# A two-layer attention and mixture-of-experts kernel: all loops written out, and four steps of the first attention moved between engines and places

## The chip, the cores and the metric

The kernel runs on one core of a Trainium2 chip. The metric is the time of one execution in device microseconds (us); less is better. Engines are called as in the profile: PE (TensorE; PEld are its weight loads), DVE (VectorE), ACT (ScalarE), POOL (GpSimd) and SP (SyncE, which here only issues DMAs).

## The reference, cut to what matters

The input is x of 16 batches x 512 tokens x 128 columns, in fp32. Two layers follow each other; a layer adds an attention and an expert network, both of the normalised x, to x.

```
xn = layernorm(x)
h  = rmsnorm(xn) * w;  q, k = l2norm(h Wq), l2norm(h Wk);  v = h Wv        # 4 heads, 2 kv heads, 32 columns
a0 = xn + gate * (softmax(causal(temperature * q k^T)) v) Wo
e0 = xn + sum over the 2 best of 16 experts: weight * (gelu(xn W1 + b1) W2 + b2)
x  = x + a0 + e0
xn = layernorm(x)
q, k, v = rmsnorm(xn) Wq, Wk, Wv, q and k times a rotary factor            # 16 heads, 4 kv heads, 8 columns
a1 = s + s Wo,   s = softmax(q k^T / sqrt(128)) v
e1 = the best of 8 experts: (silu(xn G) * (xn U)) D
x  = x + a1 + e1
```

## The kernel before, in words

`build` runs six stages one after the other, with a barrier between them: `setup`; `layer0_attention` (to about 490 us in the trace); `group_table`, a short stage that turns the counts of tokens for each expert into a table of groups of 256 rows; `expert_ffn` for layer 0 (80 groups, to about 681 us); `layer1_attention` (to about 1660 us); a second `group_table`; and `expert_ffn` for layer 1 (40 groups, to the end). Tokens reach their expert by indirect DMAs that POOL issues.

**Order.** Each engine has its own program, written by hand; semaphores tie them together (`wait_ge`, `then_inc`). In the attention stages a `body(i, o)` does one batch, and inside it the work of later batches is woven in: `o + 1` stands for the next batch, `o + 2` for the one after it. `bodies` (L196) calls it: batches 0 to 2 written out, then a loop of 5 turns with two batches in each (3 to 12), then batches 13 to 15 written out. In the loop the wait values are worked out in registers. `expert_ffn` does the same by `pipeline`: 8 groups written out, a loop of 8 turns (layer 0) or 3 turns (layer 1) with 8 groups in each, the last 8 groups written out. SP's loads there have a loop of their own. `passed` (L73) adds a semaphore increment, an instruction of its own, between waits, and `Chain.link_apart` (L62) is `link` with such an increment behind its wait.

**First attention, one batch, by engine.** Times and lines of one period stand in the rows below.

- DVE: `normalise` of the batch before (L450, L452), `statistics` of o+2 (L345, L348), `add_output` of the batch before (L459), `heads_rows` of o+1 (q, k, v rows, L380 to L387), `choose` of o+1 (routing, L393 to L408), `kz_rows` of o+1, `normal_rows` of o+2 (L357), `slots` of o+1 (L424 to L443, the last writes `meta`), `keep_sum` (L366), `square_sums` of o+2 (L372).
- POOL: `factors` of o+1 (L529 to L534), four scatters of batch o (`scatter(o, 1)`, L544), `norms` of o+2 (L512 to L518), four scatters of o+1 (`scatter(o + 1, 0)`). A scatter needs `meta` of its batch.
- PE: score pairs 0, 1, 2 (`scores`, L695 and L698; eight to a batch, two banks in turn, so pair u waits for the exponentials of pair u-2), `output` of the batch before (L723), values 0, score pair 3, `q_columns` of o+1, score pair 4, `k_columns` of o+1, values 1, `ranks` of o+1 (L671, L672), score pair 5, `x_rows` of o+2, score pair 6, the first `project`, values 2, score pair 7, two projects, values 3, the last project. `q_columns`, `k_columns`, `x_rows` and `output` all use the PSUM bank `ps_t`.
- ACT: the exponentials of the eight pairs (L607), `qT_copy` of o+1 behind the fourth (L593), `odds` of o+1 (L599) behind the fifth, `xT_copy`, four `prj_copy` and `squares` (L586) of o+2 between and behind the rest.

`kz_rows` takes the transposed keys out of `ps_t`: four copies of 32 partitions x 512 columns, each head in its own rows. `x_rows` of the next batch waits for it (`kT_sb`), and so do the scores of that batch.

**Second attention.** 64 score tiles and 64 tiles for the row maxima in a batch on PE (L1806, L1834), maxima on DVE (L1605), exponentials on ACT (L1511).

**Expert network of layer 0.** ACT does for each group two Gelus (L1078), the store of the group before (L1087), and the load of the weights of the group eight later (L1082), whose row it reads from the table. PE does the matmuls (L1047, L1057).

Of the kernel before, what the change touches and what calls it, by code (L numbers as in the profile page):

```python
# [10 lines left out]
ALU = mybir.AluOpType  # L11
# [32 lines left out]
class Chain:  # L44
# [14 lines left out]
    def link_apart(self, ins):  # L59

        self.n += 1
        ins.then_inc(self.sem, 1)  # L62
        self.eng.wait_ge(self.sem, self.base + self.n)
        passed(self.eng, self.passed)

    def end(self):
        assert self.n == self.per, (self.sem, self.n, self.per)


def passed(eng, count):  # L70


    eng.sem_inc(count, 1)  # L73
# [143 lines left out]
def layer0_attention(nc, k, x_d, base_d, meta_d, xs_d):  # L217


    with ExitStack() as ctx:  # L220
# [72 lines left out]
        with nc.Block() as block:  # L293

            @block.sync
            def _(sp):
                def load(i, o):
                    b, h, p = batch(i, o)
                    sp.wait_ge(x_used, b + 1)
                    passed(sp, k.passed_sp)  # L300
                    sp.dma_start(x[:, p], x_d[bass.ds(b * L, L), :].rearrange("(t p) d -> p t d", p=P)).then_inc(x_in[p], 16)

                def store_meta(i, o):
                    b, h, p = batch(i, o)
                    sp.wait_ge(meta_ready, b + 1)
                    passed(sp, k.passed_sp)
                    sp.dma_start(meta_d[bass.ds(b * P, P), :], meta[:, p]).then_inc(meta_out[p], 16)

                def store_base(i, o):
                    b, h, p = batch(i, o)  # L310
                    sp.wait_ge(wo_used, b + 3)
                    passed(sp, k.passed_sp)
# [21 lines left out]
            def _(dve):  # L334
# [4 lines left out]
                def statistics(i, o):  # L339
# [6 lines left out]
                    ln.link_apart(last)  # L346
# [43 lines left out]
                def choose(i, o):  # L390

                    b, h, p = batch(i, o)
                    heads.link_apart(nc.vector.tensor_tensor(lg[:], prj[:, :, QKV0:PRJ0],  # L393
# [3 lines left out]
                    heads.link_apart(last)  # L397
# [11 lines left out]

                def kz_rows(i, o):  # L410

                    b, h, p = batch(i, o)
                    dve.wait_ge(kT_ps, b + 1)
                    for head in range(H0):
                        r = slice(head * DH0, (head + 1) * DH0)
                        last = nc.vector.tensor_copy(kz[r, p, head, :], ps_t[r, :])
                    last.then_inc(kT_sb, 1)
# [44 lines left out]
                def body(i, o):  # L462
# [24 lines left out]
                kz_rows(0, 0)  # L487
# [10 lines left out]
            def _(pool):  # L498
# [3 lines left out]
                def norms(i, o):  # L502
# [8 lines left out]
                    passed(pool, k.passed_pool)  # L511
# [3 lines left out]
                    ln.link_apart(nc.gpsimd.tensor_tensor(tmp4[:, 2], tmp4[:, 1], mv[:, :, 1], ALU.mult))  # L515
# [5 lines left out]
                def factors(i, o):  # L521
# [7 lines left out]
                    fc.link_apart(nc.gpsimd.tensor_tensor(ftmp[:, 0], ss[:], bc, ALU.mult))  # L529
# [8 lines left out]
                def scatter(i, o, c):  # L538
                    b, h, p = batch(i, o)
                    if c == 0:  # L540
                        pool.wait_ge(meta_ready, b + 1)
                        passed(pool, k.passed_pool)
# [5 lines left out]
                def body(i, o):  # L548
# [12 lines left out]
                scatter(0, 0, 0)  # L561
                bodies(pool, body)
# [4 lines left out]
            def _(act):  # L567
# [26 lines left out]

                def odds(i, o):
# [14 lines left out]
                def body(i, o):  # L610
# [6 lines left out]
                    if nxt:  # L617
# [1454 lines left out]
```

## Time and profile before

| what | us |
|---|---|
| median of 3 runs (lowest, highest) | 1857.05 (1851.42, 1863.5) |
| the profiled execution, its own time | 1872.54 |
| its span, first to last instruction | 1870.8 |
| PE busy in the span | 1590.7 (85%) |
| DVE busy | 1231.6 (66%) |
| ACT busy | 939.0 (50%) |
| POOL busy | 831.1 (44%) |

Busy shares are means over stages with different limits, so the stages are read apart. Matmuls are pipelined and their ends are modelled, so a busy PE is not PE at its peak. PEclk is the granted clock as a share of 2.4 GHz.

### The profile page before, as it was taken

How to read it: one execution, taken by the hardware profiler on the slowest of the kernel's cores; microseconds unless marked ns; L12 is line 12 of the kernel's file. 1: busy time of each engine (PE TensorE's matmuls, PEld its weight loads, DVE VectorE, ACT ScalarE, POOL GpSimd, SP SyncE). 2: the span in 40 equal slices, each digit the busy share in tenths (PEclk: the TensorE clock that was granted, in tenths of full speed). 3: DMA queues.
4: the chain of work that ended last, by engine and by line, in shares of the span. 5: the costliest groups of instructions: out<-in, count | busy, mean ns of one | idle time of the engine just before them, and what ended most of it. 6: DMA issues, size and time to landing. Idle time of an engine off the chain costs nothing. (4 is left out here: it accounts for less than half of the span.)

```text
span 1870.8 us, 35103 instructions
## 1 busy us (share of the span) xinstructions
PE 1590.7 (85%) x9488; PEld 825.8 (44%) x9488; DVE 1231.6 (66%) x3176; ACT 939.0 (50%) x1790; POOL 831.1 (44%) x987
## 2 busy tenths in 40 slices
PE   1688888888499954899999999999999999928997
PEld 0344444444298852233333333333333333308996
DVE  4466566657333335688888797888878899714443
ACT  1233433434143321577777676776767777712221
POOL 2465566556140024555555555455545541003444
PEclk9999999999799985699999899999999999969998
DMA  2011111111399951212112222122211111028772
GB/s 64 26 38 43 38 39 40 34 45 32 116 279 280 280 157 57 60 55 61 58 53 66 66 58 58 43 63 67 66 57 49 52 57 55 13 62 285 234 240 80
DMA packets 141468, 165.01 MB, mean 88 GB/s; under 512 B 28010, under 2 KB 114154, under 8 KB 140138
## 3 DMA queue, kind: packets, MB, share of 16 engines
q1 hardware_dynamic: 86628, 70.75, 13.1%
q10 hardware_dynamic: 40912, 62.62, 11.1%
q0 software_dynamic: 13824, 30.47, 5.3%
q8 instruction: 39, 0.64, 0.1%
q14 instruction: 65, 0.53, 0.1%
HBM read 111.93 MB, written 51.30 MB: 87 GB/s over the span
## 5 line engine op out<-in xcount | busy, mean ns | idle before, releaser
L1605 DVE TENSOR_REDUCE c_mx<-c_ps_mx 128x1 f32<-128x512 f32 x1024 | 650.4, 684 | 121.9 <-PE c_ps_mx L1834 99.3
L1511 ACT ACTIVATE c_pt<-c_ps_e 128x512 f32<-128x512 f32 x1024 | 557.7, 602 | 230.4 <-PE c_ps_e L1806 222.4
L1834 PE MATMUL c_ps_mx<-c_kex,c_qst 72*128 72x512 bf16 x1024 | 405.7, 399 | 34.1 <-DVE c_mx L1605 20.7
L1806 PE MATMUL c_ps_e<-c_qst,c_kex 74*128 74x512 bf16 x1024 | 396.1, 389 | 1.7 <-ACT c_pt L1511 1.0
L1819 PE MATMUL c_ps_v<-c_pt,c_vp 128*32 128x512 f32 x2048 | 280.6, 621 | 1.1 <-ACT c_pt L1511 0.7
L1834 PEld LDWEIGHTS c_ps_mx<-c_kex,c_qst 72*128 72x128 bf16 x1024 | 101.8, 99 | 355.4 <-DVE c_mx L1605 225.7
L1343 POOL DMA_INDIRECT c_gy<-ys,mt x128 | 124.0, 969 | 295.8 <-issue 161.8
L607 ACT ACTIVATE a_pt<-a_ps_s,temp 128x1024 f32<-128x1024 f32 (+3 forms) x128 | 112.7, 883 | 182.6 <-PE a_ps_s L698 110.4
L1047 PE MATMUL f_ps_h<-f_xT,f_w 128*128 128x256 f32 x800 | 195.5, 384 | 0.0
L695 PE MATMUL a_ps_s<-a_qT,a_kz 128*128 128x128 f32 (+3 forms) x512 | 181.7, 472 | 0.0
L544 POOL DMA_INDIRECT xs<-a_xn,a_meta x128 | 129.2, 1010 | 109.5 <-DVE a_meta L443 75.7
L1047 PEld LDWEIGHTS f_ps_h<-f_xT,f_w 128*128 128x128 f32 x800 | 144.7, 193 | 15.0
L1057 PE MATMUL f_ps_y<-f_w,f_h 128*128 128x128 f32 x1120 | 149.4, 280 | 1.0 <-ACT f_h L1078 0.2
L1057 PEld LDWEIGHTS f_ps_y<-f_w,f_h 128*128 128x128 f32 x1120 | 139.5, 192 | 19.3 <-ACT f_h L1078 12.9
L1441 POOL DMA_INDIRECT rows<-c_row,c_bsl x64 | 63.7, 996 | 158.2 <-PE c_ps_v L1819 127.1
L1806 PEld LDWEIGHTS c_ps_e<-c_qst,c_kex 74*128 74x128 bf16 x1024 | 101.3, 99 | 73.7 <-ACT c_pt L1511 15.0
L1003 POOL DMA_INDIRECT out<-f_y,f_x x80 | 76.6, 957 | 127.3 <-DVE f_y L1130 114.8
L1078 ACT ACTIVATE f_h<-f_ps_h,f_w 128x256 f32<-128x256 f32 x160 | 67.1, 470 | 97.3 <-PE f_ps_y L1057 63.6
L695 PEld LDWEIGHTS a_ps_s<-a_qT,a_kz 128*128 128x128 f32 x512 | 81.5, 198 | 60.9 <-issue 51.4
L1074 ACT ACTIVATE f_g<-f_ps_h 128x256 f32<-128x256 f32 x120 | 46.0, 383 | 118.1 <-PE f_ps_h L1047 98.9
L1134 DVE TENSOR_TENSOR f_y<-f_ps_y,f_w 128x256 f32<-128x256 f32 x80 | 34.0, 425 | 104.8 <-PE f_ps_y L1057 104.8
L1035 PE MATMUL f_ps_x<-ident,f_x 128*128 128x128 f32 x240 | 47.3, 280 | 59.7 <-DMA f_x<-rows 37.7
(231 smaller groups left out, 1990.9 us busy)
## 6 DMA issues: line engine op xcount, KB each, us to landing
f_w<-in_we ACTq DMA_DIRECT2D x80, 321.0 KB, 4.0
f_w<-in_we ACTq DMA_DIRECT2D x40, 576.0 KB
c_qst<-qparts SPq DMA_DIRECT2D x45, 384.0 KB
f_x<-rows SPq DMA_DIRECT2D x40, 257.0 KB
f_x<-xs SPq DMA_DIRECT2D x80, 128.0 KB, 3.9
ys<-f_y ACTq DMA_DIRECT2D x80, 128.0 KB, 3.6
qparts<-c_qp SPq DMA_DIRECT2D x16, 384.0 KB
c_kex<-kparts SPq DMA_DIRECT2D x48, 96.0 KB
```

Of the source, the lines that this page charges most:

```text
L544: nc.gpsimd.indirect_dma_start(xs_d, bass.IndirectOffsetOnAxis(ap=meta[:, p, c * NT + t:c * NT + t + 1], axis=0), xn[:, p, t, :], None).th ...
L607: nc.scalar.activation(pt[:, kt % 2, 2 * pr:2 * pr + 2, 0:n], ps_s[:, u % 2, :, 0:n], ACT.Exp, bias=k.temp[:, 3:4], scale=k.temp[:, 1:2]). ...
L695: nc.tensor.matmul(ps_s[:, u % 2, j, 0:L - kt * P], kz[:, p, head, kt * P:(kt + 1) * P], qT[:, p, kt * P:L], start=True, stop=False)
L1003: nc.gpsimd.indirect_dma_start(ys_d, bass.IndirectOffsetOnAxis(ap=x[:, q, t, 2 * D:ROW].bitcast(U32), axis=0), y[:, q, t, :], None).then_i ...
L1047: last = nc.tensor.matmul(ps_h[u][:, n, :], w[:, q, col:col + P], xT[:, q % 2, :], start=True, stop=True)
L1057: last = nc.tensor.matmul(ps_y[q % 2][:, t * D:(t + 1) * D], h[:, q % 2, c, t * P:(t + 1) * P], w[:, q, col:col + D], start=c == 0, stop=c ...
L1343: nc.gpsimd.indirect_dma_start(gy[:, p, n, :], None, ys_d, bass.IndirectOffsetOnAxis(ap=mt[:, p, n:n + 1], axis=0)).then_inc(gathered[p], 16)
L1511: nc.scalar.activation(pt[:, s % 4, hl, :], ps_e[:, ring_bank(p, n)], ACT.Exp, scale=QSCALE).then_inc(exp_done, 1)
L1605: nc.vector.tensor_reduce(mx[:, g % 2, n % 16:n % 16 + 1], ps_mx[:, ring_bank(p, n)], AX, ALU.max).then_inc(mx_done, 1)
L1806: nc.tensor.matmul(ps_e[:, ring_bank(p, n)], kex[:, p, hl, kt * P:(kt + 1) * P], qst[:, p, HL * g + hl, :], start=True, stop=True).then_in ...
L1819: last = nc.tensor.matmul(ps_v[32 * hl:32 * (hl + 1), :], vp[:, p, kt, hl, :], pt[:, s % 4, hl, :], start=kt == 0, stop=kt == NT - 1)
L1834: nc.tensor.matmul(ps_mx[:, ring_bank(p, n)], qst[0:SROW, p, HL * g + hl, qt * P:(qt + 1) * P], kex[0:SROW, p, hl, :], start=True, stop=Tr ...
```

## The change

Every loop is written out: `bodies` calls all 16 bodies, and `pipeline` and SP's loads in `expert_ffn` are Python loops. The wait values become constants. All calls of `passed` go, and `link_apart` becomes `link`. Four things change in the first attention alone:

```diff
 def bodies(eng, body):
-    for o in range(3):
-        body(0, o)
-    with eng.Fori(1, 6) as i:
-        body(i, 1)
-        body(i, 2)
-    for o in range(13, NB):
+    for o in range(NB):
         body(0, o)
```

DVE's body no longer copies the keys (nor does its start, where `kz_rows(0, 0)` stood behind `choose(0, 0)`); ACT does, behind the fifth exponential and ahead of `odds` (at the start, behind `qT_copy(0, 0)`):

```diff
                         choose(i, o + 1)
-                        kz_rows(i, o + 1)
...
+                def kz_copy(i, o):
+                    b, h, p = batch(i, o)
+                    act.wait_ge(kT_ps, b + 1)
+                    for head in range(H0):
+                        r = slice(head * DH0, (head + 1) * DH0)
+                        last = nc.scalar.activation(kz[r, p, head, :], ps_t[r, :], ACT.Copy)
+                    last.then_inc(kT_sb, 1)
...
                     exps(i, o, 4)
                     if nxt:
+                        kz_copy(i, o + 1)
                         odds(i, o + 1)
```

POOL's body has the norms ahead of all eight scatters of the next batch (at its start, `scatter(0, 0, 1)` now follows `scatter(0, 0, 0)`):

```diff
                     if nxt:
                         factors(i, o + 1)
-                    scatter(i, o, 1)
                     if nxt2:
                         norms(i, o + 2)
                     if nxt:
                         scatter(i, o + 1, 0)
+                        scatter(i, o + 1, 1)
```

PE's body has the output behind four score pairs, and the ranks ahead of values 1:

```diff
-                    for u in range(3):
+                    for u in range(4):
                         scores(i, o, u)
                     if prev:
                         output(i, o - 1)
                     values(i, o, 0)
-                    scores(i, o, 3)
                     if nxt:
                         q_columns(i, o + 1)
                     scores(i, o, 4)
                     if nxt:
                         k_columns(i, o + 1)
+                        ranks(i, o + 1)
                     values(i, o, 1)
-                    if nxt:
-                        ranks(i, o + 1)
                     scores(i, o, 5)
```

In the expert stages, SP's loads and the pipeline of the others:

```diff
-                with sp.Fori(1, n_grp // NBUF) as i:
+                for i in range(1, n_grp // NBUF):
...
-                with eng.Fori(1, last) as i:
+                for i in range(1, last):
```

## Rows read from the trace of the kernel before

**Rows 1.** Window, one period: length, busy PE, PEld, DVE, ACT, POOL, clock, DMA, GB/s.

```profile
286.56:313.73 27.17, 22.27 (x142) 11.29 (x141) 17.20 (x59) 10.31 (x17) 16.19 (x20) 0.94 0.13 39
```

**Rows 2.** Timeline of POOL, that period: start, us, line, [idle before <-releaser].

```profile
278.47 1.09 POOL L544 DMA_INDIRECT xs<-a_xn,a_meta  x1 [4.81 <-DVE a_meta L443]
...
282.39 0.96 POOL L544 DMA_INDIRECT xs<-a_xn,a_meta  x1 [0.30 <-issue]
286.56 0.22 POOL L529 TENSOR_TENSOR a_ftmp<-a_ss,a_r2sq 128x24 f32<-128x24 f32 x1 [3.20 <-DVE a_ss L372]
...
291.61 0.23 POOL L534 TENSOR_TENSOR a_fac<-a_ftmp,a_r 128x24 f32<-128x24 f32 x1
...
297.16 0.23 POOL L512 TENSOR_SCALAR a_tmp<-a_mv 128x4 f32<-128x4 f32 x1
...
300.69 0.20 POOL L518 TENSOR_TENSOR a_r2sq<-a_r 128x4 f32<-128x4 f32 x1
305.53 1.09 POOL L544 DMA_INDIRECT xs<-a_xn,a_meta  x1 [4.64 <-DVE a_meta L443]
```

**Rows 3.** Timeline of DVE in the same period.

```profile
292.38 0.68 DVE L380 TENSOR_TENSOR a_qn<-a_prj,a_fac 128x512 f32<-128x512 f32 x1
...
296.28 0.23 DVE L408 TENSOR_TENSOR a_ohb<-a_oh 128x64 bf16<-128x64 f32 x1
297.72 2.79 DVE L416 COPY a_kz<-a_ps_t 32x512 f32<-32x512 f32 x4 [1.21 <-PE a_ps_t L647]
301.02 1.11 DVE L357 TENSOR_SCALAR a_xn<-a_x,a_mv,a_rstd 128x128 f32<-128x128 f32 x4 [0.51 <-POOL a_r2sq L518]
...
304.54 0.16 DVE L443 CAST a_meta<-a_slotf 128x8 uint32<-128x8 f32 x1
```

**Rows 4.** Timeline of PE in the same period.

```profile
290.51 1.16 PE L723 MATMUL a_ps_t<-wo,a_attnT 128*128 128x128 f32 x8 [1.99 <-DVE a_attnT L452]
...
294.26 0.86 PE L695 MATMUL a_ps_s<-a_qT,a_kz 128*128 128x384 f32 x2
...
302.19 0.66 PE L647 MATMUL a_ps_t<-ident,a_xn 128*128 128x128 f32 x4 [2.08 <-DVE a_xn L357]
```

**Rows 5.** Windows, second attention: written-out batch, over turn's end, last, 13 together.

```profile
875.28:929.34 54.06, 53.03 (x318) 20.10 (x316) 47.94 (x114) 40.57 (x79) 30.36 (x36) 1.00 0.22 62
...
1037.83:1098.80 60.97, 57.38 (x318) 21.25 (x316) 48.53 (x115) 41.00 (x79) 30.33 (x36) 0.92 0.19 55
...
1496.67:1550.43 53.76, 53.01 (x318) 19.84 (x316) 48.31 (x115) 40.54 (x79) 25.62 (x31) 1.00 0.20 59
sum 728.93, PE 703.97 PEld 266.94 DVE 625.55 ACT 529.06 POOL 389.88; mean PE 54.15 PEld 20.53 DVE 48.12 ACT 40.70 POOL 29.99
```

**Rows 6.** Timeline of DVE where the first loop turn of the second attention ends.

```profile
1042.54 1.29 DVE L1605 TENSOR_REDUCE c_mx<-c_ps_mx 128x1 f32<-128x512 f32 x2 [3.46 <-issue]
```

**Rows 7.** Windows, 8 groups, layer 0's experts: first loop turn, third.

```profile
534.40:550.21 15.81, 15.81 (x113) 14.88 (x113) 6.13 (x16) 5.87 (x14) 7.77 (x14) 1.00 0.98 300
...
567.16:584.07 16.91, 16.77 (x113) 14.32 (x113) 6.14 (x16) 6.71 (x16) 0.00 (x0) 1.00 0.97 280
```

**Rows 8.** Window of layer 1's experts, 16 groups in two loop turns.

```profile
1757.70:1824.00 66.30, 66.30 (x418) 61.34 (x417) 32.66 (x80) 18.32 (x49) 30.55 (x33) 1.00 0.76 238
```

**Rows 9.** Timelines: first and last `factors` of the bodies; ACT's copy of `ps_t`.

```profile
71.37 0.22 POOL L529 TENSOR_TENSOR a_ftmp<-a_ss,a_r2sq 128x24 f32<-128x24 f32 x1 [2.40 <-DVE a_ss L372]
...
447.60 0.24 POOL L529 TENSOR_TENSOR a_ftmp<-a_ss,a_r2sq 128x24 f32<-128x24 f32 x1
...
296.11 0.59 ACT L593 ACTIVATE a_qT<-a_ps_t 128x512 f32<-128x512 f32 x1
```

**Rows 10.** Timeline before the first body: routing done, keys copied.

```profile
47.15 0.23 DVE L408 TENSOR_TENSOR a_ohb<-a_oh 128x64 bf16<-128x64 f32 x1
...
50.46 2.79 DVE L416 COPY a_kz<-a_ps_t 32x512 f32<-32x512 f32 x4 [3.09 <-PE a_ps_t L647]
```

**Rows 11.** Instruction queue packets in two written-out batches, 821.5 to 929.34 us.

```profile
q14 instruction: 6, 0.05, 0.2%
```

More of the change, by code:

```diff
@@ L305, in store_meta @@
                     sp.wait_ge(meta_ready, b + 1)
-                    passed(sp, k.passed_sp)
                     sp.dma_start(meta_d[bass.ds(b * P, P), :], meta[:, p]).then_inc(meta_out[p], 16)
@@ L345, in statistics @@
                         last = nc.vector.bn_stats(stats[:, t, :], x[:, p, t, :])
-                    ln.link_apart(last)
+                    ln.link(last)
                     for t in range(NT):
@@ L392, in choose @@
                     b, h, p = batch(i, o)
-                    heads.link_apart(nc.vector.tensor_tensor(lg[:], prj[:, :, QKV0:PRJ0],
+                    heads.link(nc.vector.tensor_tensor(lg[:], prj[:, :, QKV0:PRJ0],
                                                              k.br0[:].unsqueeze(1).to_broadcast([P, NT, E0]), ALU.add))
@@ L396, in choose @@
                         last = nc.vector.max(mx8[:, t, :], lg[:, t, :])
-                    heads.link_apart(last)
+                    heads.link(last)
                     for t in range(NT):
@@ L408, in choose @@
                     nc.vector.tensor_tensor(ohb[:], oh[:, 0], oh[:, 1], ALU.add).then_inc(oh_ready, 1)
[L410 to L417, printed above, removed]
                 def slots(i, o):
@@ L510, in norms @@
                         pool.wait_ge(qkv_ready, b - 1)
-                    passed(pool, k.passed_pool)
                     ln.link(nc.gpsimd.tensor_scalar(tmp4[:, 0], mv[:, :, 1], EPS_LN, None, ALU.add))
@@ L514, in norms @@
                     ln.link(nc.gpsimd.tensor_tensor(tmp4[:, 1], rstd[:], rstd[:], ALU.mult))
-                    ln.link_apart(nc.gpsimd.tensor_tensor(tmp4[:, 2], tmp4[:, 1], mv[:, :, 1], ALU.mult))
+                    ln.link(nc.gpsimd.tensor_tensor(tmp4[:, 2], tmp4[:, 1], mv[:, :, 1], ALU.mult))
                     ln.link(nc.gpsimd.tensor_scalar(tmp4[:, 0], tmp4[:, 2], 1e-6, None, ALU.add))
@@ L528, in factors @@
                     bc = r2sq[:].unsqueeze(2).to_broadcast([P, NT, H0 + KV0])
-                    fc.link_apart(nc.gpsimd.tensor_tensor(ftmp[:, 0], ss[:], bc, ALU.mult))
+                    fc.link(nc.gpsimd.tensor_tensor(ftmp[:, 0], ss[:], bc, ALU.mult))
                     fc.link(nc.gpsimd.tensor_scalar(ftmp[:, 1], ftmp[:, 0], 1e-24, None, ALU.max))
@@ L541, in scatter @@
                         pool.wait_ge(meta_ready, b + 1)
-                        passed(pool, k.passed_pool)
                     for t in range(NT):
@@ L561, in _ @@
                 scatter(0, 0, 0)
+                scatter(0, 0, 1)
                 bodies(pool, body)
@@ L639, in _ @@
                 qT_copy(0, 0)
+                kz_copy(0, 0)
                 rows(1)
@@ L1000, in put_rows @@
                     pool.wait_ge(y_sb, j + 1)
-                    passed(pool, k.passed_pool)
                     for t in range(GT):
@@ L1248, in put_k @@
                     sp.wait_ge(kl_ready, b + 1)
-                    passed(sp, k.passed_sp)
                     sp.dma_start(kparts_d[p].rearrange("j r l -> r j l"), kp[:]).then_inc(k_out[p], 16)
@@ L1254, in put_q @@
                     sp.wait_ge(ql_ready, b + 1)
-                    passed(sp, k.passed_sp)
                     sp.dma_start(qparts_d[p].rearrange("j r l -> r j l"), qp[:]).then_inc(q_out[p], 16)
@@ L1275, in q_stack @@
                     sp.wait_ge(q_out[p], 16 * (h + 1))
-                    passed(sp, k.passed_sp)
                     for a in range(3):
@@ L1295, in shift @@
                     sp.wait_ge(sh_ready, 4 * b + g + 1)
-                    passed(sp, k.passed_sp)
                     for n in range(2):
@@ L1340, in gather @@
                         pool.wait_ge(pv, 16 * (b - 3) + s + 2)
-                    passed(pool, k.passed_pool)
                     for n in rows:
@@ L1369, in norms @@
                     ln.link(nc.gpsimd.tensor_tensor(tmp4[:, 1], rstd[:], rstd[:], ALU.mult))
-                    ln.link_apart(nc.gpsimd.tensor_tensor(tmp4[:, 2], tmp4[:, 1], mv[:, :, 1], ALU.mult))
+                    ln.link(nc.gpsimd.tensor_tensor(tmp4[:, 2], tmp4[:, 1], mv[:, :, 1], ALU.mult))
                     ln.link(nc.gpsimd.tensor_scalar(tmp4[:, 0], tmp4[:, 2], float(np.finfo(np.float32).eps), None, ALU.add))
@@ L1400, in k_parts @@
                     pool.wait_ge(kT_sb, b + 1)
-                    pc.link_apart(nc.gpsimd.tensor_tensor(kr[:], k32[:], kp[:, 0, :], ALU.subtract))
+                    pc.link(nc.gpsimd.tensor_tensor(kr[:], k32[:], kp[:, 0, :], ALU.subtract))
                     pc.link(nc.gpsimd.tensor_copy(kp[:, 1, :], kr[:]))
@@ L1407, in q_parts @@
                     pool.wait_ge(qT_sb, b + 1)
-                    pc.link_apart(nc.gpsimd.tensor_tensor(qr[:], q32[:], qp[:, 0, :], ALU.subtract))
+                    pc.link(nc.gpsimd.tensor_tensor(qr[:], q32[:], qp[:, 0, :], ALU.subtract))
                     pc.link(nc.gpsimd.tensor_copy(qp[:, 1, :], qr[:]))
@@ L1418, in normal_rows @@
                         pool.wait_ge(kept_xn, b - 1)
-                    passed(pool, k.passed_pool)
                     for t in range(NT):
@@ L1429, in keep_xn @@
                     pool.wait_ge(xn_ready, b + 1)
-                    passed(pool, k.passed_pool)
                     nc.gpsimd.tensor_copy(row[:, p, :, 0:D], xn[:, p]).then_inc(kept_xn, 1)
@@ L1439, in scatter @@
                         pool.wait_ge(pv, 16 * (b + 1) + s + 2)
-                    passed(pool, k.passed_pool)
                     nc.gpsimd.indirect_dma_start(
@@ L1653, in choose @@
                     dve.wait_ge(prj_sb, NT * (b + 1))
-                    passed(dve, k.passed_dve)
                     lg = prj[:, :, QKV1:PRJ1]
@@ L1657, in choose @@
                         last = nc.vector.max(mx8[:, t, :], lg[:, t, :])
-                    pro.link_apart(last)
+                    pro.link(last)
                 def choose_index(i, o):
@@ L1696, in statistics @@
                         last = nc.vector.bn_stats(stats[:, t, :], x1[:, p, t, :])
-                    ln.link_apart(last)
+                    ln.link(last)
                 def moments(i, o):
```

16 lines of the change are left out of this document (removed).

## The prediction

> **What bounds the kernel now.** I read the page first, then windows by stage, then the timelines of one period, then the timeline of a turn's end. The chain that ended last reaches back only into the last stage, so it can't say what an edit in the first stages is worth; each stage has to be read by its own period.
>
> In the first attention no engine is full: in a period of 27.17 us PE is busy 22.3, DVE 17.2, POOL 16.2 and ACT 10.3 [rows 1]. So a ring of waits sets the period. The timelines show it. `factors` starts on POOL at 286.56 and ends at 291.84 [rows 2]. On DVE the q rows follow at 292.38, the routing ends at 296.51, then DVE waits 1.21 us for the transposed keys and spends 2.79 us on copying them; the normal rows start at 301.02 (after 0.51 us for POOL's norms), and `meta` is written by 304.70 [rows 3]. POOL's norms, behind four scatters, only ended at 300.89 [rows 2]. After the normal rows PE transposes them, projects, ACT squares, DVE sums, and the next `factors` starts 27.17 us after the last. PE stands still for 1.99 us ahead of the output [rows 4], and its clock is granted at 0.94 on average [rows 1].
>
> In the second attention PE is busy 53.0 of 54.06 us in a written-out batch. In the batch over the end of a loop turn it takes 60.97 us, with 57.4 busy at a clock of 0.92 [rows 5]. DVE stands still there for 3.46 us, and the row names no releaser but "issue" [rows 6]. There are four such turn ends in the stage, and none in the six written-out batches.
>
> In layer 0's experts the first loop turn takes 15.81 us for 8 groups with PE always busy, a later one 16.91 us [rows 7]. In that stage DMA moves 280 to 300 GB/s at a share of 0.97. In layer 1's experts PE is busy all 66.30 us of 16 groups, two turn ends included [rows 8].
>
> **The change part by part.** All sums are against the profiled execution (1872.54 us, span 1870.8), which is 0.8% over the median of 1857.05; I take the gain over unscaled, since the two differ by less than the gain's own doubt.
>
> *1. Key columns by ACT.* Four copies of 32x512 leave DVE: 2.79 us, and with them the wait of 1.21 us ahead of them [rows 3]. ACT gains four. ACT's copy of 128x512 out of the same bank took 0.59 us [rows 9]; on DVE 32x512 cost 2.79 / 4 = 0.70 each, so fewer partitions need not be cheaper. I take 4 x 0.59 = 2.4 us; the ends are 0.8 (four times the 0.2 us of ACT's smallest operations here) and twice my value, 4.7. They lie behind the fifth exponential and ahead of `odds` and the sixth. What hides them is PE's score pair 5, values 1 and the ranks, which PE does between the keys' transposes and `x_rows`; ACT is busy only 10.3 of 27.2 us. If the cover is gone (4.7 us), `x_rows` and `slots` (which needs `odds`) come some 1 to 2 us later.
>
> *2. Norms ahead of the scatters.* POOL's norms take 300.89 - 297.16 = 3.73 us. They needed only statistics that DVE has by the end of `factors`, and now follow `factors` at once: they end at F + 5.3 + 3.8 = F + 9.1 (F is the start of `factors`), instead of F + 14.3. So neither the keys nor the norms hold the normal rows: DVE starts them when routing ends.
>
> *3. The eight scatters in one piece.* The first four take 282.39 + 0.96 - 278.47 = 4.88 us, spaced by 0.96 and 0.30 idle; eight take 2 x 4.88 + 0.30 = 10.06 us [rows 2]. Behind them on POOL's queue stands the next `factors`, and DVE's q rows wait for that. Here the edit can turn against itself, so I add up the ring through POOL: `factors` 5.28; handoff 0.05; q rows to the end of routing 296.51 - 292.38 = 4.13; handoff 0.05; normal rows to `meta` 304.70 - 301.02 = 3.68; handoff to the scatter 305.53 - 304.70 = 0.83; eight scatters 10.06; handoff 0.1. Sum 24.2 us. The removed `passed` increments are worth about 0.1 us each, three of them in this ring; I leave them as margin.
>
> *4. Output behind four pairs, ranks earlier.* Pair 3 is two products of 0.86 us each with two short ones behind them, all overlapping in part, about 1.6 us, and it moves into the 1.99 us in which PE waited for the output's input [rows 4]. It needs the exponentials of pair 1, which are done by then. The values 0 behind it lose nothing. The keys' transposes had ended when DVE began to copy them, at 297.72 or F + 11.2 [rows 3]; 1.6 us earlier is F + 9.6. The ranks now stand ahead of values 1 and wait for the end of routing at F + 9.5, so they cost nothing.
>
> The PE ring: `x_rows` started at 302.19, F + 15.6, after a wait of 2.08 us [rows 4]. PE was ready for it at F + 13.5 and is now at F + 11.9, with the normal rows done at F + 10.7 (they start at F + 9.5 and take 1.1). What follows, to the next `factors`, took 27.17 - 15.6 = 11.5 us, and a mean clock of 0.94 means that 0.06 x 27.17 = 1.6 us of a period are lost to the half clock. That makes 23.4 us, or 21.8 with that loss gone; PE's own busy time of 22.3 is in between. It is shorter than POOL's 24.2, so POOL's ring is late next, and it sets the period.
>
> First attention: from the first to the last `factors` 447.60 - 71.37 = 376.23 us in 14 periods, 26.87 each [rows 9]; at 24.2 that is 338.8, a gain of 37.4. At the start, routing ends at 47.38 and then DVE waited 3.09 us for the keys and copied for 2.79 us before the statistics of batch 1 [rows 10]. Now these start at once: norms end at 53.4, `meta` of batch 0 at 57.1, eight scatters from 57.9 to 68.0, so the second `factors` starts at 68.1 instead of 71.37: 3.3 us. The tail gives 0.7. Sum 41 us.
>
> *5. Loops of the second attention.* 13 batches took 728.93 us; written-out ones took 53.76 to 54.06 (four of them among these, mean 53.9) [rows 5]. 13 x 53.9 = 700.7, so 28 us go, if the new code runs like the written-out code that is there: 3.5 us of standstill at four turn ends, and about as much again of half clock behind each. The upper end is 29; the lower is 0, if what DVE waits for at a turn's end is met once in a batch anyway.
>
> The Trainium skill (Runtime: NRT & Kernel Launch, "Instruction fetch mechanics") says that an engine holds two pages of instructions and fetches ahead in sequence only, so that a taken branch out of them stalls for a fetch, while straight code hides it. The 3.46 us fit. Another page (Advanced Engine Details and Errata, "Control Flow Timing") gives about 0.1 us for a compare-and-branch; by that alone the four turn ends were worth 0.4 us and the sum would be 28 us smaller. The trace speaks for the first.
>
> *6. Loops of layer 0's experts.* Eight turns; the first took 15.81, the other seven about 16.93 each. The first shows that DMA can carry that pace (300 GB/s) [rows 7]. What slows the others is ACT, which does two Gelus and two DMA issues per group with registers worked out between, and is late for PE after the written-out start's lead is used up. 7 x (16.93 - 15.81) = 7.8 us at most, 0 at least (DMA share 0.97); I take 7, nearer to the first turn's row since nothing in it waits for a DMA.
>
> *7. Layer 1's experts.* PE never stands still [rows 8]: 0. Barriers, tables and `setup` are untouched: 0. The other `passed` increments lie beside longer waits: 0.
>
> Sum: 41 + 28 + 7 = 76 us. The profiled execution would go to 1796, the median to 1857 - 76 = 1781 us.
>
> **The rivals.**
>
> *A. The period of the first attention closes elsewhere.* The kz copies on ACT at their dear end, `odds` behind them, PE's in-order wait for the ranks, or half clock on PE keep the period at 26 to 27. For it: the orders of four engines are moved at once, and PE has 22.3 busy of 27. Against it: the sums above. Part 4 and 1 to 3 then give 5 to 15 us instead of 41: 1857 - 35 - 10 = 1812. Chance 0.2.
>
> *B. POOL's ring is not as long as that*, since some of the handoffs overlap, and PE's sets 22.6, the middle of its bounds: 14 x 1.6 = 22 us more, 1759. Against it: every link of the sum is an in-order step. Chance 0.07.
>
> *C. Straight code stalls for its instructions: slower.* Where a loop turn reused what an engine held, written-out code must bring in each piece once, and POOL, DVE or ACT stands still for it in the middle of the chain. For it: the loop code of the first attention and of layer 0's experts ran hundreds of us with next to none of those transfers, and in layer 0's experts they would queue behind a DMA share of 0.97. Against it: the two written-out batches of the second attention brought in 6 packets of instructions on one of the two queues [rows 11] and show no standstill over 0.9 us. Price: one standstill with its half clock is (728.93 - 700.7) / 4 = 7.1 us per attention batch, for 16 to 20 batches that were in loops, and 3.5 us per 8 groups in 11 turns: 20 x 7.1 + 11 x 3.5 = 180 us at most, against 76 won. It decides the sign once some 42% of them lie bare; at 60%, 1781 + 108 = 1889 us. Chance 0.06.
>
> *D. The loops alone give nothing* (the stall at a turn's end only moves to other places, as many as before), while the first attention gains its 41: 1857 - 41 = 1816. For it: the DVE row says "issue", not what it waited for. Against it as for C. Chance 0.07.
>
> **How the numbers follow.** The forecast has 0.6: 1781 us. The range reaches to rivals A and D on one side and nearly to B on the other: 1760 to 1822; outside are C, most of B, and a stall or two in many places. A measurement of this kernel can tell about 1% (18.6 us) from no change. The forecast, A, B and D all lie more than 1% below 1857, though A and D could join: 0.88 faster, 0.06 within 1%, 0.06 slower.
>
> **What would show it.** Right: `factors` of successive batches 24.2 us apart, on POOL directly behind the eighth scatter with no idle for DVE's sums; normal rows directly behind the routing on DVE, with no wait; four ACT copies of about 0.6 us; batches of the second attention all at 53.8 to 54.1 us with a clock of 1.00; the 80 groups 1.97 us apart. Wrong: a period of 26 or more, with the wait ahead of `x_rows` still there; standstills of 3 us with "issue" on DVE or ACT in the middle of written-out bodies; groups at 2.05 us or more, with DMA as releaser.

## The result, and the profile after

| | median us (lowest, highest), runs |
|---|---|
| before | 1854.24 (1850.62, 1863.5), 4 |
| after | 1770.33 (1767.86, 1775.95), 4 |
| ratio after to before | 0.9544, 95% interval 0.9501 to 0.9588 |
| profiled execution after | 1775.95, span 1774.2 |

The kernel became 84 us faster; 1781 had been forecast, inside 1760 to 1822. The time came out nearly right in part by luck: the largest term of the sum, 41 us for the first attention's orders, measured 22 to 25, and the increments, which were put at nothing, measured 25 to 28. The loops were sized rightly.

The period of the first attention, from one `factors` to the next, is now 23.46 us. The window has the columns of [rows 1].

```profile
254.07:277.53 23.46, 20.73 (x145) 11.24 (x143) 14.41 (x55) 12.86 (x21) 16.43 (x19) 1.00 0.15 47
```

POOL's timeline of that period answers to [rows 2].

```profile
254.07 0.24 POOL L496 TENSOR_TENSOR a_ftmp<-a_ss,a_r2sq 128x24 f32<-128x24 f32 x1
...
259.04 0.23 POOL L501 TENSOR_TENSOR a_fac<-a_ftmp,a_r 128x24 f32<-128x24 f32 x1
...
263.33 0.20 POOL L485 TENSOR_TENSOR a_r2sq<-a_r 128x4 f32<-128x4 f32 x1
267.41 1.27 POOL L510 DMA_INDIRECT xs<-a_xn,a_meta  x1 [3.88 <-DVE a_meta L413]
268.98 0.96 POOL L510 DMA_INDIRECT xs<-a_xn,a_meta  x1 [0.30 <-issue]
...
276.56 0.95 POOL L510 DMA_INDIRECT xs<-a_xn,a_meta  x1 [0.30 <-issue]
277.53 0.24 POOL L496 TENSOR_TENSOR a_ftmp<-a_ss,a_r2sq 128x24 f32<-128x24 f32 x1
```

DVE's timeline answers to [rows 3].

```profile
259.30 0.69 DVE L359 TENSOR_TENSOR a_qn<-a_prj,a_fac 128x512 f32<-128x512 f32 x1 [1.08 <-POOL a_fac L501]
...
262.98 0.23 DVE L387 TENSOR_TENSOR a_ohb<-a_oh 128x64 bf16<-128x64 f32 x1
263.56 1.11 DVE L336 TENSOR_SCALAR a_xn<-a_x,a_mv,a_rstd 128x128 f32<-128x128 f32 x4 [0.36 <-POOL a_r2sq L485]
...
266.95 0.16 DVE L413 CAST a_meta<-a_slotf 128x8 uint32<-128x8 f32 x1
...
274.44 0.95 DVE L351 TENSOR_REDUCE a_ss<-a_sq 128x24 f32<-128x768 f32 x1 [6.73 <-ACT a_sq L553]
```

The new `factors` starts as the eighth scatter ends, with no idle, though DVE's sums have been there since 275.39: POOL's ring closes the period. It can be added up in these rows: `factors` and norms up to the normal rows 9.49, normal rows to `meta` 3.55, handoff 0.30, eight scatters 10.10. The keys no longer stand on DVE, and what holds the normal rows is 0.36 us of the norms. ACT's copies:

```profile
263.46 2.37 ACT L568 ACTIVATE a_kz<-a_ps_t 32x512 f32<-32x512 f32 x4
```

PE's timeline of the period ([rows 4]) has three waits left, and none ahead of the output or of `x_rows`; the clock of the window is 1.00.

```profile
261.05 0.66 PE L625 MATMUL a_ps_t<-ident,a_qn 128*128 128x128 f32 x4 [1.77 <-DVE a_v L366]
267.50 0.72 PE L640 MATMUL a_ps_p<-w,a_xnT 128*128 128x272 f32 x2 [0.29 <-ACT a_xnT L539]
271.13 0.70 PE L640 MATMUL a_ps_p<-w,a_xnT 128*128 128x272 f32 x2 [0.58 <-ACT a_prj L547]
```

The other stages, as windows of the same kernel: 8 groups of layer 0's experts; two ordinary batches of the second attention; its one odd batch.

```profile
530.00:545.80 15.80, 15.80 (x114) 14.98 (x113) 6.05 (x17) 6.84 (x16) 0.00 (x0) 1.00 1.02 304
810.40:863.91 53.51, 52.95 (x318) 20.10 (x316) 47.83 (x114) 40.43 (x79) 30.35 (x36) 1.00 0.21 63
...
1023.77:1076.78 53.01, 52.73 (x318) 20.17 (x316) 47.75 (x114) 40.44 (x79) 30.38 (x36) 1.00 0.22 64
1076.78:1135.90 59.12, 57.25 (x318) 21.05 (x316) 48.28 (x115) 40.95 (x79) 29.98 (x35) 0.91 0.20 57
```

The experts answer to [rows 7]: every 8 groups take 15.80 us now, at 304 GB/s. The batches answer to [rows 5]: 53.0 to 53.5 us and no turn's end. In the odd one POOL waits 4.29 us for gathered rows (2.6 on average in the two batches before it), DVE then 1.80 us for POOL, PE 1.59 us for DVE, and the clock falls. Of the nine other kernels below with all loops written out, eight took 53.2 to 54.4 us for the same batch and one 58.4. What delays those rows stays open.

### The profile page after: what moved, and what is told of

Its sections match the earlier page's. It is cut to its first block and busy times, and to the rows that moved or that the text cites. A ratio compares the mean times of both kernels' runs of the same rounds, so it can differ in the third digit from the quotient of the medians.

```text
span 1774.2 us, 29893 instructions
## 1 busy us (share of the span) xinstructions
PE 1545.9 (87%) x9488; PEld 819.9 (46%) x9488; DVE 1183.1 (67%) x3112; ACT 974.2 (55%) x1853; POOL 835.1 (47%) x987
## 5 line engine op out<-in xcount | busy, mean ns | idle before, releaser
L1794 PE MATMUL c_ps_mx<-c_kex,c_qst 72*128 72x512 bf16 x1024 | 401.5, 394 | 17.4 <-issue 8.5
L1766 PE MATMUL c_ps_e<-c_qst,c_kex 74*128 74x512 bf16 x1024 | 392.0, 385 | 1.7 <-ACT c_pt L1472 1.6
L1779 PE MATMUL c_ps_v<-c_pt,c_vp 128*32 128x512 f32 x2048 | 276.7, 612 | 1.1 <-ACT c_pt L1472 0.7
L673 PE MATMUL a_ps_s<-a_qT,a_kz 128*128 128x128 f32 (+3 forms) x512 | 175.3, 461 | 0.0
L1032 PEld LDWEIGHTS f_ps_y<-f_w,f_h 128*128 128x128 f32 x1120 | 144.0, 192 | 6.3
L1032 PE MATMUL f_ps_y<-f_w,f_h 128*128 128x128 f32 x1120 | 144.3, 275 | 0.0
```

The lines of the kernel that those rows point to most:

```text
L673: nc.tensor.matmul(ps_s[:, u % 2, j, 0:L - kt * P], kz[:, p, head, kt * P:(kt + 1) * P], qT[:, p, kt * P:L], start=True, stop=False)
L1032: last = nc.tensor.matmul(ps_y[q % 2][:, t * D:(t + 1) * D], h[:, q % 2, c, t * P:(t + 1) * P], w[:, q, col:col + D], start=c == 0, stop=c ...
L1766: nc.tensor.matmul(ps_e[:, ring_bank(p, n)], kex[:, p, hl, kt * P:(kt + 1) * P], qst[:, p, HL * g + hl, :], start=True, stop=True).then_in ...
L1779: last = nc.tensor.matmul(ps_v[32 * hl:32 * (hl + 1), :], vp[:, p, kt, hl, :], pt[:, s % 4, hl, :], start=kt == 0, stop=kt == NT - 1)
L1794: nc.tensor.matmul(ps_mx[:, ring_bank(p, n)], qst[0:SROW, p, HL * g + hl, qt * P:(qt + 1) * P], kex[0:SROW, p, hl, :], start=True, stop=Tr ...
```

## The experiments

All times are medians, ratios are to runs of the kernel before made on the same chip in the same set (medians 1852 to 1856 us). Single executions of the kernel before spread from 1850 to 1870 us, those of a changed one by 2 to 9, so differences between medians are good to a few us. "Period" is the mean over the fourteen between the second `factors` and the last; the second attention is counted from its first batch's slots to its last batch's.

**The kernel before once more.** Its first profiled execution was 18 us above the median, so I wanted a second profile.

> The kernel before once more, for a second profile. The first profiled execution took 1872.5 us where the median of all is 1855. Theory: what differs is how often PE falls to half clock: the first attention's period is 27.1 us with such a stretch and 25.55 without one, and the first profile has twelve with and two without; at a time near 1855 some ten of fourteen or fewer have one, or the turn ends of the second attention cost less. Rival: the same twelve, and the difference lies in the second attention alone (batches over 59 us).

It took 1852.56 us, and here every second period keeps its full clock. Two successive periods as windows:

```profile
250.17:276.39 26.22, 22.81 (x144) 11.78 (x143) 17.12 (x59) 10.84 (x17) 15.99 (x20) 0.93 0.13 40
276.39:301.32 24.93, 21.19 (x143) 11.07 (x142) 17.19 (x59) 10.41 (x17) 16.20 (x19) 1.00 0.14 42
```

The first `factors` of the bodies is at 71.58 and the last at 430.00: a mean of 25.60 where the profile that I had read has 26.87 [rows 9]. That is 17.8 of the 20.0 us between the two executions; the second attention adds 6.3 (874.9 against 868.6), and what follows it gives 4.7 back. The period that I had taken as typical [rows 1] is one with the clock down, and twelve of fourteen were such; this one, near the median, has seven.

**Loops and increments, each alone.** First the kernel before with every loop written out and the increments gone, orders as before:

```
-    with eng.Fori(1, 6) as i:
-        body(i, 1)
-        body(i, 2)
+    for o in range(NB):
+        body(0, o)
...
-    eng.sem_inc(count, 1)
+    pass
```

> The kernel before with every loop written out and no added increments; the first attention keeps its old orders (keys on DVE, four scatters ahead of the norms, output behind three pairs). Theory: the loops are worth 33 us in the second attention (batches at 53.1) and 8 us in layer 0's experts (groups at 1.97), and in the first attention only the increments in its ring count: periods fall from 26.9 to about 26.4, 7 us. Time about 1854 - 48 = 1806 us. Rival (the loops are most of the change, also in the first attention): periods of 24 or less there and a time of 1780 or less.

1795.82 us, ratio 0.9678 (0.9636 to 0.9721). Period 24.81 (24.44, and 26.01 in the three with a lower clock) where 26.4 had been expected, from the profile with twelve such periods; second attention 834.4, experts 15.80 per 8 groups.

Then the same with the increments kept:

> The kernel before with all loops written out and nothing else: orders as before and every passed increment kept. Theory (loops and increments add up): the second attention's batches at 54.1 to 54.5 us, its thirteen 845 us from first to last, layer 0's experts 15.8 us per 8 groups; in the first attention the period is the 24.4 to 24.8 of the run with loops out and increments gone, plus the 0.75 us that increments cost with the new orders: 25.2 to 25.6. Time 1795.8 + 10 + 11 = about 1817 us. Rival (the turn's end costs the first attention nothing; what shortened its period there was that the increments went): period stays 26.9, so 14 x 1.3 = 18 us more, 1835 us. Second rival (increments hide behind DVE's and PE's waits in the old order): 24.4 to 24.8, 1807 us.

1820.68 us, ratio 0.9786 (0.9731 to 0.9842): the sum of loops and increments nearly as the first theory had it (1817). The second attention took 849.4 us; in the first the period is 25.66 (24.86 and 26.33 in turn), as good as the 25.60 of the second profile of before. So the loops cost the first attention nothing, which was the rival's thesis; its 1835 us came from the period of 26.87.

**The orders alone**, loops and increments kept:

> The kernel before with the four moved steps of the first attention alone; loops and increments stay. Theory: periods of the first attention fall to the sum of POOL's ring with its increments, about 24.2 us, a gain of 41 us, and the other stages stay as before (four turn ends in the second attention, batches of 54): about 1813 us. Rival (the orders pay only with straight code, since the wait values in registers lengthen the handoffs): periods of 25.5 or more, 1830 us or more.

1842.83 us, ratio 0.9934 (0.9909 to 0.9958), where 1813 had been expected. The period is 24.55 (24.01 at best, six of fourteen with a lower clock), not 24.2. The last `factors` is at 411.85 instead of 430.00, but the second attention took 884.4 us instead of 868.6, with batches over a turn's end of 61.4 to 63.7 us instead of 58.6 to 61.2 in the two profiles of before. No instruction of that stage was changed. Why its turn ends became dearer is open. With the loops kept, then, the orders are worth 12 us.

**The changed kernel with all increments back**, then with those of one group of engines:

```
+def passed(eng, count):
+    eng.sem_inc(count, 1)
...
+                    passed(pool, k.passed_pool)
```

> The kernel after with all semaphore increments between waits put back. Theory: the increments are what my sums missed: each costs several tenths of a us where it stands between a wait and the work, so the first attention's period rises from 23.47 to about 24.2 (10 us) and a batch of the second attention from 53.1 to 53.9 (12 us): 1770 + 22 = 1792 us. Rival (they cost about 0.1 us, as the prediction had it, and the constants in place of registers did the rest): 1774 us at most, periods of 23.6 and batches of 53.2.

1798.77 us, ratio 0.9703 (0.9658 to 0.9748): 28 us given back, 22 had been expected. POOL's and DVE's timelines of that kernel around `factors`, `meta` and the first scatters:

```profile
260.64 0.24 POOL L513 TENSOR_TENSOR a_ftmp<-a_ss,a_r2sq 128x24 f32<-128x24 f32 x1
261.07 0.28 POOL L514 TENSOR_SCALAR a_ftmp<-a_ftmp 128x24 f32<-128x24 f32 x1 [0.20 <-POOL a_ftmp L513]
...
274.70 1.09 POOL L528 DMA_INDIRECT xs<-a_xn,a_meta  x1 [4.42 <-DVE a_meta L429]
276.10 0.96 POOL L528 DMA_INDIRECT xs<-a_xn,a_meta  x1 [0.30 <-issue]
```

```profile
273.72 0.16 DVE L429 CAST a_meta<-a_slotf 128x8 uint32<-128x8 f32 x1
```

From the end of `meta` to the second scatter it is 276.10 - 273.88 = 2.22 us, and 268.98 - 267.11 = 1.87 without increments. From the first operation of `factors` to the second it is 0.43 and 0.33 (254.07 to 254.40). The period is 24.00 to 24.04 in eleven of fourteen.

> The changed kernel with the passed increments back on POOL alone. In the run with all of them back, meta to the second scatter took 2.22 us instead of 1.87, factors and norms 0.1 us more each, and two of 0.1 us on DVE lay in the 0.36 us that DVE waits for the norms. Theory (those of POOL are the ones that cost): period 24.0 us, + 8 us in the first attention, the second attention's batches at 54 us like with all of them, about 1795 us. Rival (the costs are spread over the three engines): period 23.7, batches at 53.5, 1782 us.

> The changed kernel with the passed increments back on SP and DVE and none on POOL. Theory: DVE's two lie in its wait for the norms and SP's loads are early, so the period stays at 23.47 to 23.5 and the second attention at 53.1 to 53.4 a batch: 1770 to 1774 us. Rival (DVE's chain in the second attention is PE's supplier, SP's reloads of k and q stand in it): batches 53.6 to 54, 1778 to 1785 us.

POOL alone: 1797.8 us, ratio 0.9697 (0.9661 to 0.9733). SP and DVE alone: 1771.98, ratio 0.956 (0.9526 to 0.9594). So the whole 28 us are POOL's, and those of the other two cost nothing that shows. In the second attention the waits of DVE say how; over three batches with POOL's increments:

```profile
DVE c_mx L1600 <- PE c_ps_mx L1829: 13.8, 30, 0.8
DVE c_stats L1691 <- POOL c_x L1353: 2.3, 3, 1.2
```

and with those of SP and DVE, the same three batches:

```profile
DVE c_mx L1600 <- PE c_ps_mx L1829: 13.7, 30, 0.8
```

The columns are us in total, times, longest. POOL's combined rows `c_x` come late once a batch, 0.77 us each time; DVE waits for them in order ahead of the maxima that PE waits for. A batch there takes 53.55 to 54.24 us where it takes 53.22 to 53.45 without.

**One turn's end instead of four.** Before, with only two loop turns in each attention:

```
-    with eng.Fori(1, 6) as i:
+    with eng.Fori(1, 3) as i:
         body(i, 1)
         body(i, 2)
-    for o in range(13, NB):
+    for o in range(7, NB):
         body(0, o)
```

> The kernel before with batches 3 to 6 in two loop turns and 7 to 12 written out, in both attentions: one turn end in each where the kernel before has four, registers and increments as before, and the loops of the experts as before. Theory (the cost is the turn's end, not the registers): second attention first to last 875 - 3 x 7 = about 853 us, one batch of 59 to 61 us, the looped ones without a turn's end 54.1 to 54.5; first attention between 26.9 and the 25.7 us of the run with loops out. Time about 1855 - 21 - 9 = 1825 us. Rival (written-out code stalls as often for its instructions): 1850 to 1856 us. Second rival (working out addresses in registers is what costs): the written-out batches 53.5 and below, the looped ones 54.5 and above.

1835.52 us, ratio 0.9904 (0.9869 to 0.9939). Windows of the second attention: a looped batch inside a turn, the one over the turn's end, two behind it; below, DVE's row at the turn's end.

```profile
961.26:1015.44 54.18, 52.97 (x318) 20.09 (x316) 47.87 (x115) 40.33 (x78) 30.37 (x36) 1.00 0.22 63
1015.44:1076.65 61.21, 57.33 (x318) 21.35 (x316) 48.53 (x115) 41.06 (x79) 30.34 (x36) 0.92 0.19 55
1076.65:1130.75 54.10, 52.96 (x318) 20.10 (x316) 47.87 (x115) 40.67 (x79) 30.38 (x36) 1.00 0.21 62
1130.75:1184.52 53.77, 53.02 (x318) 19.91 (x316) 48.01 (x114) 40.55 (x79) 30.37 (x36) 1.00 0.22 63
```

```profile
1020.20 1.29 DVE L1605 TENSOR_REDUCE c_mx<-c_ps_mx 128x1 f32<-128x512 f32 x2 [3.51 <-issue]
```

The looped batch is within 0.4 us of the written-out ones, so addresses in registers cost next to nothing here, and one turn's end costs 7 us in the one place where it stands. The second attention took 851.9 us, 16.6 less than in the second profile of before: 5.5 us for each turn's end taken out. That is all that this kernel gained; the 1825 us expected had another 9 in the first attention. The Trainium skill (Runtime: NRT & Kernel Launch, "Instruction fetch mechanics") says that a taken branch out of the two pages that an engine holds stalls for a fetch. The 3.51 us at the turn's end fit, and so does their absence from straight code. What the instruction queues did fits too. In the kernel before, around the turn's end of [rows 6] (1038 to 1044 us), one of them moved three packets (columns: packets, MB, share), and as many in this kernel from 1016 to 1022 us:

```profile
q14 instruction: 3, 0.02, 1.0%
```

In the loop of the first attention, from 205 to 415 us of the kernel before, neither queue moved a packet, and there a turn's end costs nothing. So it is not the branch as such that costs. That DVE stood still for these packets is not shown: the rows tell neither whose they are nor what the engine waited for. The first attention's period of 25.79 is that of an ordinary execution of before.

**The orders, each undone in the changed kernel.** The keys back on DVE:

```
+                        kz_rows(i, o + 1)
...
-                        kz_copy(i, o + 1)
```

> The changed kernel with the four key copies back on DVE between routing and the normal rows. Theory (the copies stand in the POOL ring: factors, routing, keys, normal rows, meta, eight scatters): the period grows from 23.47 by the 2.8 us of the copies and by what DVE waits for the keys, to 26.2 to 26.8; POOL still has no idle ahead of factors but waits for meta 2.8 us longer; 14 x 2.8 = 39 us and 3 at the start, about 1812 us. Rival (the ring through PE and ACT binds as well, so that taking ACT's copies away gives some of it back): period 24.5 to 25.5, about 1790 us.

1830.74 us, ratio 0.9844 (0.9789 to 0.9899), 60 us slower than the changed kernel. Windows of two successive periods:

```profile
263.71:289.78 26.07, 20.95 (x145) 11.24 (x144) 17.27 (x59) 10.75 (x17) 16.44 (x19) 1.00 0.14 42
289.78:317.71 27.93, 23.69 (x145) 12.85 (x144) 17.27 (x59) 10.73 (x17) 16.44 (x19) 0.88 0.13 39
```

At full clock the ring grows by 2.6 us, a little less than expected (2.7 to 3.3, for a time of 1812 us). The rest, which neither theory had, is the clock: PE now waits 3.32 us for `a_v`, and all but four periods have a lower clock, at 1.4 to 1.9 us each. 6 us more go before the second `factors`.

POOL's old order:

```
                         factors(i, o + 1)
+                    scatter(i, o, 1)
                     if nxt2:
                         norms(i, o + 2)
                     if nxt:
                         scatter(i, o + 1, 0)
-                        scatter(i, o + 1, 1)
```

> The changed kernel with POOL's old order (scatters of the second half behind factors, then norms, then four scatters of the next batch). Theory: norms end at F + 5.2 + 0.3 + 4.9 + 3.7 = F + 14, so the normal rows start no sooner than in the run with loops out, where POOL's norms were the last thing that they waited for at a period of 24.44; the period is 24.1 to 24.5 here, the start about 2 us later: 1770 + 12 + 2 = about 1784 us. Rival (with the keys off DVE the scatters in two halves are better than in one): POOL waits for DVE's sums and the period is under 23.4, 1768 us or less.

1791.73 us, ratio 0.9641 (0.9587 to 0.9695). At full clock the period is 24.44, as expected and to the hundredth that of the run with old orders throughout; five of fourteen are 26.01 to 26.20, which the expected 1784 us left out. DVE, with no keys to copy, waits for the norms instead, and PE for DVE:

```profile
229.54 1.11 DVE L336 TENSOR_SCALAR a_xn<-a_x,a_mv,a_rstd 128x128 f32<-128x128 f32 x4 [3.83 <-POOL a_r2sq L485]
```

```profile
230.71 0.66 PE L624 MATMUL a_ps_t<-ident,a_xn 128*128 128x128 f32 x4 [2.06 <-DVE a_xn L336]
```

PE's old order:

> The changed kernel with PE's old order (output behind three score pairs, ranks behind values 1). Theory: POOL's ring of 23.47 us holds without a wait for DVE's sums (they are ready 2.1 us before factors starts), PE waits 1 to 2 us ahead of output and is later by that, which the 2.1 us absorb: period 23.5 and 1770 to 1773 us. Rival (PE's wait ahead of the output adds to its ring and half clock comes back with it): period 24.2 to 25, 1781 to 1790 us.

1773.61 us, ratio 0.9531 (0.9479 to 0.9583). The period is 23.70, 0.23 more; PE waits 1.00 us ahead of the output and 0.74 ahead of the q columns, together the 1.77 that it now waits in one piece.

**A third slot for `xn`**, so that POOL can do norms first and still scatter in two halves behind `factors` (shown in part; reads of `xn` and DVE's wait for a free slot go by the batch modulo 3):

```
-        xn = sb("a_xn", [P, 2, NT, D])
+        xn = sb("a_xn", [P, 3, NT, D])
...
                         norms(i, o + 2)
+                    scatter(i, o, 1)
                     if nxt:
                         scatter(i, o + 1, 0)
-                        scatter(i, o + 1, 1)
```

> The kernel after with a third buffer for the normal rows, and POOL's order factors, norms, the second four scatters of this batch, the first four of the next. So only four scatters lie between a batch's slots and the next factors. Theory (POOL's ring sets the period of 23.47; the sums on DVE are ready 2.1 us before POOL takes them): the period falls to about 21.5 to 22 and the time by 14 x 1.5 to 2.0 us, to about 1746 us. Rival (PE's ring or PE's own work is as long): period 23.2 or more, 1767 us or more.

1752.21 us (1751.75 to 1753.72), ratio 0.9443 (0.9402 to 0.9483): 18 us faster than the changed kernel (1746 had been expected). A period as window, and POOL's row that opens one:

```profile
242.49:264.79 22.30, 20.73 (x143) 11.26 (x142) 14.31 (x55) 12.87 (x21) 16.20 (x19) 1.00 0.16 49
```

```profile
220.19 0.22 POOL L497 TENSOR_TENSOR a_ftmp<-a_ss,a_r2sq 128x24 f32<-128x24 f32 x1 [2.82 <-DVE a_ss L352]
```

With the eight scatters no longer between `meta` and `factors`, POOL waits 2.82 us for DVE's sums, and the ring through PE, ACT and DVE sets 22.30 us.

## Why the prediction was right, and where it was not

The time can be split up along several ways:

| medians, us | increments in | increments out |
|---|---|---|
| loops, old orders | 1855.6 | not run |
| loops, new orders | 1842.8 | not run |
| straight, old orders | 1820.7 | 1795.8 |
| straight, new orders | 1798.8 | 1770.3 |

By way of the straight kernels, loops are worth 34.9 us, increments 24.9 or 28.4, orders 21.9 or 25.5. The parts don't simply add: with the loops kept the orders give 12.8, and loops taken out behind them 44.1. I had 28 + 7 for the loops, which measured 35; 41 for the orders, which measured 22; and nothing for the increments, which measured 28. The two errors nearly cancel; the forecast, 11 us off (3 of them the median of before, which moved), had one term 19 too large and one 28 too small. That they cancelled is luck.

*The increments* are the term of the sum that failed. Step 3 left them as a margin of 0.1 us each, and step 7 said that they lie beside longer waits: 0. One between two dependent operations on POOL does cost 0.1 us (0.43 against 0.33). The one ahead of the scatters costs 0.35, and it stands in the ring; with 0.1 for that of `factors` and 0.1 for norms, which are now the last thing the normal rows wait for, that is the 0.56 us between 23.46 and 24.02. Up to the last `factors` it is 12.6 us (407.44 against 394.88): 7.8 of these by 14 periods, 2.1 ahead of the second `factors`, and the rest mostly in a last period of 26.49 us with a lower clock. In the second attention I looked for cover engine by engine and did not ask who waits for POOL: 0.77 us per batch on DVE, and the stage is 9 to 15 us longer with POOL's increments (846.0 against 836.4, 849.4 against 834.4). My POOL ring of 24.2 us was, term by term, that of a kernel with increments, and such a kernel measured 24.0; the handoff of 0.83 us from `meta` to scatter [rows 2, 3], which I took as given, was mostly the increment (0.30 without, and a first scatter 0.18 us longer, so 0.35 in all).

*Step 1* held: 2.37 us for the copies (2.4 taken), hidden on ACT. *Step 2* held to 0.4 us: norms end at F + 9.46, not 9.1, so they and not the routing release the normal rows, which start at F + 9.49 as forecast. *Step 3's* mechanism held exactly: POOL's ring, no idle ahead of `factors`, eight scatters in 10.10 us (10.06). The second `factors` came 5.0 us earlier (66.33 against 71.37) for 3.3; it is at 68.41 with the increments. *Step 4* came out smaller than I described it: PE is freed, but POOL's ring hides all but 0.23 us of it. And the 1.99 us ahead of the output, which it was to fill, are those of the first profile; in the second profile of before, as with PE's old order in the changed kernel, that wait is 1.0. Its bounds for PE's ring (21.8 to 23.4) were sound: where a third slot opened POOL's ring, 22.30 us came out.

The three edits to DVE and POOL are one. With POOL's old order the keys on ACT bring no shorter full-clock period (24.44 with and without, DVE waits 3.83 us for norms); with the new order and the keys on DVE the kernel is slower than with all three old (1830.7 against 1795.8).

*What the gain of the first attention was reckoned from* was wrong too. 41 us came from a period of 26.87 us, of one profiled execution 18 us above its median. An ordinary one has 25.60, and the stage gains 430.00 - 394.88 = 35 us, of which 12.6 are the increments. The profile was not scaled down for this, on the ground that 0.8% was within the gain's doubt; but the excess was not spread over the kernel, it lay in the two stages that the change shortens, 17.8 us of it in the first attention, with the clock.

*The clock.* Step 4 priced it from the mean of 0.94: 1.6 us lost per period. That is what a period with it costs here (26.01 against 24.44, 26.33 against 24.86). It comes, roughly, with PE's longer waits. Ahead of `x_rows`: seven to twelve of fourteen periods before, with waits of up to 2.08 us [rows 4]; five with 2.06 us; three with 1.57. Ahead of the q columns, with at most 1.3 us ahead of `x_rows`: ten with 3.32 (keys on DVE), six with up to 2.6 (orders alone), three with up to 2.1 (all increments back); none with 1.77, 0.74 or 0.60. That PE's wait is the cause was not tried by itself. Where POOL's ring is in front a stretch costs little: with all increments back three fall into the stage, in periods of 24.01, 24.24 and 26.49 us.

*Step 5* forecast 28 us from loops alone. Turn ends were worth 19 us against the second profile and 25.5 against the first (849.4 us with increments kept), since they cost 4 to 7 us each and not always 7.1. Batches then went from 54.2 to 53.3 through the increments. *Step 6*: 8.0 us for 7; the groups run at the first turn's pace as the rows suggested. That ACT was late for PE in the looped groups is borne out: from 550.21 to 660 us of the kernel before PE's weight loads waited for its Gelus as below (us in total, times, longest), and in the run with only the loops out they don't.

```profile
PEld f_ps_y L1057 <- ACT f_h L1078: 11.4, 40, 0.6
```

The two terms together make 27 or 33.5 us by the profiles, and 34.9 by the medians; what is missing between them is open.

*Step 7*, layer 1's experts: 158.75 us from first to last group before, 158.76 after, as [rows 8] said.

*The rivals.* A did not come: no period of 26, PE's wait for the ranks cost nothing. B was right about PE's ring and wrong that it would set the period. C, straight code that stalls, is refuted: no standstill with "issue" of that size on DVE or ACT in straight bodies, though the queues of instructions moved more (packets, MB, share; the whole kernel before, then the whole changed kernel). The one odd batch is the only doubt, and its rows name a DMA of gathered rows.

```profile
q8 instruction: 39, 0.64, 0.1%
q14 instruction: 65, 0.53, 0.1%
...
q8 instruction: 78, 1.28, 0.3%
q14 instruction: 78, 0.64, 0.1%
```

D's "loops give nothing" was false in the second attention and in the experts, and true in the first attention.

## What to carry to other kernels

Price every instruction that a change deletes on the engine whose ring sets the period, bare semaphore increments too, and for each handoff that is far longer than its neighbours ask what stands in it. Before taking a gain from one profile, see how far that execution is from the median and in which stage the excess lies. Edits to a ring of several engines have no value of their own (here the same four orders were worth 12, 22 or 25 us, by what stood beside them): undo each alone in the new kernel, and look for the slot (here a third buffer) that separates the two rings.

## What the hardware showed that I had not expected

- A bare increment on POOL, behind a wait, costs 0.10 us between dependent operations (0.43 against 0.33) and 0.35 us ahead of an indirect DMA's issue (2.22 against 1.87). All of SP's and DVE's together cost less than can be told (1771.98 against 1770.33).
- A stretch at the lower of PE's two clock levels (1.2 instead of 2.4 GHz) costs 1.3 to 1.6 us of a period where PE stands in the ring that sets it (mean clock 0.93 or 0.94; 1.9 at 0.88), and nothing where POOL's ring is in front (24.01 at 0.93). In a program whose period is steady otherwise it can come in every second one (24.86, 26.33, 24.87, 26.33); the kernel before had it in seven periods of fourteen in one execution and in twelve in another.
- A turn's end of the second attention's loop costs DVE 3.5 us of standstill, and the batch 4 to 7 us. The first attention, with the same loop form, loses nothing to it (25.66 without loops, 25.60 with), and no packet of instructions moved in 210 us of its loop.
